# Additive attention with half-length key tiles for the first query blocks, and tanh units that begin after twelve of sixteen neighbourhood-attention rounds

## The chip, the cores and the metric

One NeuronCore of one Trainium2 chip. The metric is the time of one execution on the device, in microseconds (us). The profile is of one such execution; its times count from the first recorded instruction. The engines are TensorE (PE), VectorE (DVE), ScalarE (ACT), GpSimd (POOL) and SyncE (SP, which here only issues DMAs). Each runs its own list of instructions in order, and they wait for each other through semaphores.

## What is computed

Two images of 32 x 32 tokens with 128 channels, all in float32. Three layers follow one another:

```python
# 1: neighbourhood attention, 7 x 7, 8 heads of 16 channels
attn = einsum('bijnd,bijnpqd->bijnpq', q, k_neighbours) + bias
out = softmax(attn) @ v_neighbours
y = layernorm(x + (out @ proj_w + proj_b) * gate) * ln_g + ln_b
# 2: additive attention over all 1024 tokens of an image, 32 hidden units
t = layernorm(y)
q, k = t @ Wt, t @ Wx
e = (tanh(q[:, :, None, :] + k[:, None, :, :] + bh) * Wa).sum(-1) + ba
y = y + softmax(e) @ t
# 3: mixture of 8 experts, top 1, capacity 320
out = y + expert(layernorm(y)) * probability
```

The second layer needs 2 x 1024 x 1024 x 32 = 67 million tanh values. They are the largest work of the kernel.

## The kernel before

**Blocks.** The 2048 tokens are 16 blocks of 128 (`NB`), 8 to an image (`BPI`); blocks 0 to 7 are image 0.

**Rounds of the first layer.** A block takes two rounds (`NR` = 32; even heads, odd heads). Round `rho` is: scores on PE (L601), bias and row minimum on DVE (L1125), the exponential on ACT (L986), transposes of the probabilities on PE, their copies out of PSUM, and the product with the values on PE (L648). After a block's second round come the head sums, their inverse spread over the channels, the output projection and the gated sum `gate_heads` (L1188), which leaves the block in `y_all`. A round has 320 keys for most blocks and 256 for the first and the last block of an image.

**Layernorms.** Two layernorms stand between the first layer and the second. They are done for groups of blocks, and each is a chain of small instructions on DVE: `row_stats` (L1205, L1208), then `scale_start` and `scale_end` (L1214, L123 to L135), an inverse square root in 12 linked steps on 128 x 4 numbers. Scaling the rows themselves is on DVE (L1229, L1236) or on POOL (`scale_rows`, `weigh_rows`, `normal_rows`, L461 to L483). Then the tokens are transposed (`turn_tokens`, L757), copied to `xT`, and multiplied into keys (`key_half`, L762, copied to `k4` and left in PSUM too) and queries (`query_columns`, L769, copied to `q4`).

**Units of the second layer.** A unit `t` (0 to 127; 8 to a block, `CH`) is four columns of `q4` (each holds four queries, with their 32 hidden units, on the 128 partitions), each against the 1024 keys of the image: one tile of 128 x 4096 in a ring of three (`ring`, in `front`). POOL and DVE form the sums of key and query (`key_query_sums`, L507 and L1323): POOL reads the keys from SBUF, DVE from PSUM. In image 0 POOL makes two tiles of 1024 and two of 512, DVE two of 512; in image 1 POOL makes two of 1024 and one of 512, DVE one of 512 and one of 1024. ACT does one tanh over the whole tile (`hidden_units`, L1049). PE multiplies by `Wa` into banks 0 and 1 of PSUM (`energies`, L801); it waits for `h_ready`, and both makers of sums wait for `h_used` of three units earlier. PE may start a new block only when DVE has taken the energies of the last one out (`least_ready`, `least`, L1330).

**Finishing a block.** When the 8 units of block `p` are done: `least` on DVE, exponential on ACT (L1053), eight transposes (L813), copies (L1338), the product with the tokens (`attend`, L822), then `attended`, `normed`, `route` and `slotted` on DVE with three small products on PE, and on POOL an indirect DMA that puts the block's rows where their expert reads them (`scatter`, L515). These steps are spread over the ten steps behind the block's end (`query_block(t, phase)`).

**Order of the work.** It is written out by hand. First come the sixteen rounds of image 0 (`for rho in range(RPI)` on PE, ACT and DVE). Then comes a passage in which blocks 4 to 7 are normalised on DVE, image 1's queries and keys for the first layer are projected, and the keys and queries of image 0 for the second layer are made. Then one loop over steps `t` follows on each engine; step `t` holds unit `t`'s tanh and energies, the sums of unit `t + 2`, and whatever small functions give for `t`: rounds 16 to 31 begin at every third step,

```python
def begin(rho):
    return PACE * (rho - RPI - 1)
```

so at steps -3, 0, 3, ... 42. Blocks 8 to 11 are normalised in steps 29 to 38 (`middle`), blocks 12 to 15 in steps 49 to 58 (`late_rows`). After the loop the experts run (L926 to L946, L1079, L1519), in which nothing is changed.

**Memory.** Queries, keys and values of the first layer lie in `front` for image 0 and in `late` for image 1. `front` is also the ring, so no sum can be made before round 15 has been used up (`pv_done, RPI`).

## Time and profile before

| | |
|---|---|
| median of 3 runs | 742.11 us (741.74 to 746.65) |
| the profiled execution's own time | 744.08 us |
| its span, first to last instruction | 741.9 us |
| mean granted TensorE clock (1 is 2.4 GHz, 0.5 is 1.2 GHz) | 0.913 |
| first tanh of a unit starts | 109.79 us |
| last tanh ends | 659.9 us |
| busy share of the span: PE, DVE, ACT, POOL | 77%, 75%, 78%, 63% |

The span less the two tanh times leaves three parts: 109.8 us ahead of the units, 550.1 us of units, 82.0 us behind them. The time of an instruction on DVE, ACT or POOL is from its start to its end in the record; two that follow each other overlap a little, so that the distance from start to start is shorter (a tanh lasts 3.6 us and the next starts 3.5 us after it).

### The profile page before, as it was taken

The numbers are of one execution on the slowest core, as the hardware profiler recorded it, in microseconds if no ns is written. First come the engines' busy times: TensorE is split into PE (matmuls) and PEld (weight loads), VectorE is DVE, ScalarE is ACT, GpSimd is POOL, SyncE is SP. The second block draws the span as 40 slices with busy tenths as digits, with TensorE's granted clock in tenths as the row PEclk, the third lists the DMA queues.
The fourth block names the chain that finished last, engine by engine and source line by source line (L and its number), as shares of the span: only waits on it lengthen the run. The fifth ranks groups of instructions, "written<-read, shape, count | busy, mean of one in ns | idle before, by whom it ended". The sixth has DMA issues, their size and how long they took to land.

```text
span 741.9 us, 12240 instructions
## 1 busy us (share of the span) xinstructions
PE 570.2 (77%) x4496; PEld 272.5 (37%) x4496; DVE 555.0 (75%) x1444; ACT 577.5 (78%) x368; POOL 470.6 (63%) x539
## 2 busy tenths in 40 slices
PE   6999858798999868899447666766767668768994
PEld 3666423243434323343113131222222212328783
DVE  3768765768897768878987788798798786853356
ACT  3777539998999767899457899999999999960541
POOL 2000228976888668788835788788888886830464
PEclk9999968999999869999858899999999998986998
DMA  8500000000000000007000000000000000001400
GB/s 322 175 1 2 1 0 2 0 2 4 9 4 10 3 9 5 1 12 285 21 4 8 4 11 2 12 9 4 12 10 4 12 8 5 6 7 25 133 22 28
DMA packets 13819, 22.22 MB, mean 30 GB/s; under 512 B 1264, under 2 KB 11026, under 8 KB 12992
## 3 DMA queue, kind: packets, MB, share of 16 engines
q1 hardware_dynamic: 12352, 18.53, 7.3%
q0 software_dynamic: 1408, 2.91, 1.2%
q8 instruction: 36, 0.59, 0.3%
q14 instruction: 23, 0.19, 0.1%
HBM read 14.70 MB, written 7.37 MB: 30 GB/s over the span
## 4 chain that ended last, share of the span: by engine, by line
PE 36%; DVE 27%; issue 18%; ACT 13%; POOL 4%; DMA 0%; DVEq 0%; POOLq 0%; SPq 0%; ACTq 0%
PE ps L801 12%; ACT front L1049 11%; DVE front L1323 7%; POOL front L507 4%; PE ps L601 3%; PE ps L946 3%; PE ps L936 2%; PE ps L648 2%; PE ps L822 2%; DVE back L1125 2%; PE ps L630 2%; PE ps L639 2%; DVE lnw L134 1%; PE ps L813 1%; DVE rec L1362 1%
## 5 line engine op out<-in xcount | busy, mean ns | idle before, releaser
L507 POOL TENSOR_SCALAR front<-k,q 128x1024 f32<-128x1024 f32 (+1 forms) x448 | 410.9, 936 | 129.0 <-PE ps L801 110.7
L1049 ACT ACTIVATE front<-front 128x4096 f32<-128x4096 f32 x128 | 456.2, 3608 | 41.8 <-DVE front L1323 23.6
L801 PE MATMUL ps<-front,cst 128*32 128x512 f32 x2048 | 277.1, 648 | 74.8 <-ACT front L1049 61.1
L1323 DVE TENSOR_SCALAR front<-ps,q 128x512 f32<-128x512 f32 (+1 forms) x256 | 213.5, 877 | 34.6 <-PE ps L801 27.9
L801 PEld LDWEIGHTS ps<-front,cst 128*32 128x32 f32 x2048 | 53.1, 114 | 173.6 <-issue 85.2
L986 ACT ACTIVATE back<-back,mn 128x320 f32<-128x320 f32 (+1 forms) x128 | 62.5, 537 | 20.2 <-DVE mn L1125 20.2
L1125 DVE CUSTOM_DVE_ANT_0 back<-ps,back 128x320 f32<-128x320 f32 (+1 forms) x128 | 54.0, 468 | 12.8 <-PE ps L601 11.8
L464 POOL TENSOR_SCALAR y_all<-y_all,lny,lnc 128x128 f32<-128x128 f32 x8 | 3.5, 444 | 69.0 <-DVEq L1224 69.0
L1338 DVE COPY ptm<-ps 128x512 f32<-128x512 f32 x32 | 22.1, 689 | 30.1 <-PE ps L813 30.1
L1152 DVE COPY back<-ps 128x512 f32<-128x512 f32 x44 | 30.2, 687 | 16.3 <-PE ps L639 13.9
L639 PEld LDWEIGHTS ps<-cst,back 128*128 128x128 f32 x176 | 20.0, 150 | 44.0 <-issue 31.6
L832 PE MATMUL ps<-cst,rec 128*128 128x128 f32 x16 | 5.9, 371 | 38.0 <-DVE rec L1362 38.0
L822 PEld LDWEIGHTS ps<-x_one,ptm 128*128 128x128 f32 x256 | 31.4, 199 | 10.0 <-issue 8.8
L822 PE MATMUL ps<-x_one,ptm 128*128 128x129 f32 x256 | 34.3, 289 | 0.8 <-DVE ptm L1338 0.8
L515 POOL DMA_INDIRECT xbuf<-rec,slots x16 | 16.3, 1019 | 29.2 <-DVEq L119 25.9
L639 PE MATMUL ps<-cst,back 128*128 128x128 f32 x176 | 31.3, 303 | 2.2 <-DVE back L1152 2.0
L543 POOL DMA_INDIRECT out<-back,dest x20 | 19.9, 993 | 17.6 <-DVE back L1529 13.4
L630 PE MATMUL ps<-cst,back 128*128 128x128 f32 x176 | 27.3, 287 | 1.7 <-ACT back L993 1.7
L601 PE MATMUL ps<-late 32*128 32x320 f32 (+1 forms) x128 | 26.7, 494 | 2.5 <-DVE mn L1125 1.7
L813 PEld LDWEIGHTS ps<-cst,pm 128*128 128x128 f32 x128 | 14.7, 151 | 32.8 <-issue 19.2
L813 PE MATMUL ps<-cst,pm 128*128 128x128 f32 x128 | 22.9, 306 | 4.7 <-ACT pm L1053 2.0
L1072 ACT ACTIVATE front<-ps 128x384 f32<-128x384 f32 (+1 forms) x8 | 3.1, 434 | 29.8 <-PE ps L926 29.8
(140 smaller groups left out, 701.4 us busy)
## 6 DMA issues: line engine op xcount, KB each, us to landing
back<-in_w SPq DMA_DIRECT2D x2, 2048.0 KB, 10.3
xbuf<-rec SPq DMA_DIRECT2D x1, 2720.0 KB, 14.4
front<-xbuf SPq DMA_DIRECT2D x2, 720.0 KB, 7.2
back<-in_inner SPq DMA_DIRECT2D x1, 1280.0 KB, 9.8
back<-in_b SPq DMA_DIRECT2D x1, 1280.0 KB, 14.1
xT<-in_xT SPq DMA_DIRECT2D x4, 256.0 KB, 5.4
back<-in_top SPq DMA_DIRECT2D x1, 1024.0 KB, 6.8
back<-in_bottom SPq DMA_DIRECT2D x1, 1024.0 KB, 14.9
```

The source lines that it names most:

```text
L507: last = nc.gpsimd.tensor_scalar(ring[t % 3][:, c, lo:hi], k4[:, img * L + lo:img * L + hi], q4[:, m:m + 1], 1.0, ALU.add, ALU.mult)
L601: return nc.tensor.matmul(bank(to, 0, n), q_par[img][r][rows, at * P:(at + 1) * P], kT[img][rows, k0:k0 + n], start=True, stop=True)
L630: last = nc.tensor.transpose(bank(turn_bank(rho, c), g * P, (g + 1) * P), prob[r][:, g, c * P:(c + 1) * P], c_("ident"))
L639: last = nc.tensor.transpose(bank(4, g * P, (g + 1) * P), prob[rho % 2][:, g, c * P:(c + 1) * P], c_("ident"))
L801: last = nc.tensor.matmul(bank(half)[c * U:(c + 1) * U, :], c_("wa", U - QPG - QPG * s, 2 * U - QPG - QPG * s), ring[t % 3][:, c, half * 5 ...
L813: last = nc.tensor.transpose(bank(4, k * P, (k + 1) * P), pm[:, (4 * half + k) * P:(4 * half + k + 1) * P], c_("ident"))
L822: last = nc.tensor.matmul(bank(6, 2 * P, 2 * P + C + 1), ptm[:, k, :], x_one[:, p // BPI * BPI + k, :], start=(k == 0), stop=(k == BPI - 1))
L986: nc.scalar.activation(prob[r][:, g, 0:n], nlog[r][:, g, 0:n], ACT.Exp, bias=mn[r][:, g:g + 1], scale=-1.0).then_inc(p_ready, 1)
L1049: nc.scalar.activation(ring[t % 3], ring[t % 3], ACT.Tanh).then_inc(h_ready, 1)
L1125: nc.vector.tensor_tensor_reduce(out=nlog[r][:, g, 0:n], in0=bank(frm, 0, n), in1=btab[kind][:, 2 * g + r, :], scale=-1.0, scalar=3e38, op ...
L1152: nc.vector.tensor_copy(pts[rho % 2][:, c, :], bank(4)).then_inc(turn_copied, 1)
L1323: last = nc.vector.tensor_scalar(ring[t % 3][:, c, lo:hi], ps[:, at + lo:at + hi], q4[:, m:m + 1], None, ALU.add)
```

## The change

Four things are changed together.

1. **Twelve rounds first (`RS` = 12).** Only rounds 0 to 11 (blocks 0 to 5) run ahead of the loop. The other twenty begin at the steps of a table: rounds 12 to 15 at -6, -3, 0 and 2, rounds 16 to 23 every four steps from 7 to 35, rounds 24 to 31 every three from 38 to 59.
2. **Half the keys at a time.** The first four blocks of an image are worked in two passes. Units 0 to 15 take blocks 0 to 3 (four units each) against keys 0 to 511; units 16 to 31 take the same blocks against keys 512 to 1023; then blocks 4 to 7 follow as before with 8 units each. Image 1 does the same from unit 64 on. A half unit has eight columns of `q4` against 512 keys, again 128 x 4096. Its sums are eight tiles of 512: six on POOL and two on DVE in image 0, five and three in image 1. After the first pass `least` keeps the negated energies in `pmh` and their minimum in `nmh`; after the second one it takes the smaller of both minima, and ACT does two exponentials of 512 instead of one of 1024. The first pass of a block ends without the other finishing steps; those of blocks 0 to 3 follow each other every 4 units, behind units 19, 23, 27 and 31 (and 83 to 95).
3. **Layernorms and keys in other places.** Blocks 0 to 3 are normalised in rounds 8 to 11 (statistics, `scale_start` and `scale_end` of the first layernorm all stand in rounds 8 and 9) and not in rounds 9 to 15. Blocks 4 to 6 are normalised in steps 7 to 11 of the loop, on DVE and POOL, block 7 alone in steps 11 and 12, on DVE, in place of the passage between rounds and loop. Tokens and keys of blocks 4 to 7 follow at step 14 (`KEYS_1`), on PE and DVE; unit 16 is the first to need them. Blocks 8 to 11 now stand at steps 45 to 54 and blocks 12 to 15 at 66 to 75, the keys of blocks 8 to 11 at step 61 (`KEYS_2`).
4. **One store for queries, keys and values (`conv`)** instead of two, so that the ring is free from the start; image 1's projections stand in steps 4 to 6 (`ENTRY`), partly on DVE, its values in steps 7 to 9.

The core of the diff (the functions that only follow from it, such as the counts of semaphores, are left out):

```diff
-PACE = 3
+RS = 12
+BS = RS // 2
...
+BEGIN = dict(zip(range(RS, NR), [-6, -3, 0, 2] + [7 + 4 * k for k in range(8)] + [38 + 3 * k for k in range(8)]))
+ROWS_STEPS = (7, 8, 9)
+ENTRY = 4
+KEYS_1, TOKENS_2, KEYS_2 = 14, 58, 61
...
+for _img in range(B):
+    for _half in range(2):
+        for _k in range(BPH):
+            GROUPS.append(Group(_img * BPI + _k, _half, len(GROUPS) and GROUPS[-1].last + 1, CH // 2))
+    for _k in range(BPH, BPI):
+        GROUPS.append(Group(_img * BPI + _k, None, GROUPS[-1].last + 1, CH))
...
+def tiles_of_unit(u):
+
+    g = GROUPS[GROUP_AT[u]]
+    k = u - g.first
+    base = g.block * U
+    if g.half is None:
+        return [(c * L, 0, L, base + c * CH + k, k, c) for c in range(QPG)]
+    return [(n * HL, g.half * HL, HL, base + n % QPG * CH + 2 * k + n // QPG, 2 * k + n // QPG, n % QPG)
+            for n in range(2 * QPG)]
...
+        def pool_part(u, n):
+
+            g = GROUPS[GROUP_AT[u]]
+            if g.half is not None:
+                return (0, HL) if n < (6 if g.block < BPI else 5) else (0, 0)
+            if g.block < BPI:
+                return (0, L) if n < 2 else (0, HL)
+            return (0, L) if n < 2 else (0, HL) if n == 2 else (0, 0)
...
+                if t == 8:
+                    scale_rows(2, 4, 7)
+                    weigh_rows("lng", ALU.mult, 4, 7)
+                    weigh_rows("lnb", ALU.add, 4, 7, done=True)
+                if t == 11:
+                    normal_rows(2, 4, 7)
...
-            for rho in range(RPI):
-                if rho + 1 < RPI:
+            for rho in range(RS):
+                if rho + 1 < RS:
                     scores(rho + 1)
...
+                if t == KEYS_1:
+                    pe.wait_ge(n_ready, NG * (RPI + 2))
+                    turn_tokens(1, 2)
+                    query_columns(1, 3)
+                    pe.wait_ge(dve_sums, NEW_KEYS[1])
+                    key_half(1, 5)
...
+                if rho == 8:
+                    dve.wait_ge(y_ready, 3)
+                    row_stats(0, 3)
                 if rho == 9:
                     dve.wait_ge(y_ready, 4)
-                    row_stats(0, 2)
+                    row_stats(3, 4)
+                    scale_start(0, 4)
+                    scale_end(0, 4, ln_scale)
                 if rho == 10:
-                    row_stats(2, 4)
+                    dve.wait_ge(ln_rows, 1)
+                    row_stats(0, 4)
                 if rho == 11:
                     scale_start(0, 4)
...
-            row_stats(4, BPI - 1)
-            gated(BPI - 1)
-            dve.wait_ge(y_ready, BPI)
-            row_stats(BPI - 1, BPI)
-            scale_start(4, BPI)
-            scale_end(4, BPI)
-            normal_rows(y_all, 4, BPI)
-            weigh_rows(4, BPI)
-            row_stats(4, BPI)
-            scale_start(4, BPI)
-            scale_end(4, BPI)
-            normal_rows(x_all, 4, BPI)
-            dve.sem_inc(t_ready[1], 1)
+                    scale_end(0, 4, ln_last)
...
+                if t == project_step(6) + 1:
+                    dve.wait_ge(misc_read, misc_uses(t))
+                    row_stats(4, 7)
+                    scale_start(4, 7)
+                    scale_end(4, 7, ln_scale)
...
+                if g.half == 0:
...
+                    nc.vector.tensor_tensor_reduce(out=pmh[:, k, :], in0=bank(p % 2), in1=c_("ba").broadcast_to([P, HL]),
+                                                   scale=-1.0, scalar=3e38, op0=ALU.add, op1=ALU.min,
+                                                   accum_out=nmh[:, k:k + 1]).then_inc(least_ready, 1)
+                    return
```

How the lists of instructions move, at the places that matter. ACT ahead of its first tanh; before (`late` is the first layer's store of image 1):

```order
L999 ACTIVATE ots<-ps 128x256
L969 ACTIVATE late<-ps,sbq 128x512 x2
L974 ACTIVATE late<-ps,cst 128x512
L1003 ACTIVATE xT<-ps 128x512
L969 ACTIVATE late<-ps,sbq 128x512 x2
L1007 ACTIVATE k<-ps 128x512
L974 ACTIVATE late<-ps,cst 128x512
L1003 ACTIVATE xT<-ps 128x512
L1007 ACTIVATE k<-ps 128x512
L1044 ACTIVATE q<-ps,cst 128x256
L986 ACTIVATE back<-back,mn 128x256 x4
L1049 ACTIVATE front<-front 128x4096 x2
```

and after (L1067 are the exponentials of rounds 12 and 13, L1118 is the tanh):

```order
L1080 ACTIVATE ots<-ps 128x256
L1067 ACTIVATE back<-back,mn 128x320 x2
L1084 ACTIVATE xT<-ps 128x512
L1067 ACTIVATE back<-back,mn 128x320 x2
L1088 ACTIVATE k<-ps 128x512
L1145 ACTIVATE q<-ps,cst 128x128
L1067 ACTIVATE back<-back,mn 128x320 x4
L1118 ACTIVATE front<-front 128x4096 x2
```

Between the last round and the first tanh the projections of image 1 and the second half of tokens and keys are gone, and two rounds' exponentials stand there.

DVE at the layernorm of blocks 4 to 7; before, in the passage ahead of the loop (L119 ends a chain):

```order
L119 ISA
L1214 TENSOR_SCALAR lnh<-mvs 128x4
L125 TENSOR_SCALAR lnw<-lnh 128x4
L126 TENSOR_SCALAR lny<-lnw 128x4
L133 TENSOR_TENSOR lnw<-lny,lnh 128x4
L134 TENSOR_TENSOR lnw<-lnw,lny 128x4
L135 SCALAR_TENSOR_TENSOR lny<-lnw,lny 128x4
```

and after, in the loop, behind unit 9's sums (L1394) and ahead of unit 10's (L1205 is a copy of image 1's values, L1292 the heads of block 7):

```order
L1205 TENSOR_TENSOR conv<-ps,cst 128x32x16
L1292 COPY ots<-ps 128x256
L1296 BN_STATS bns<-y_all 128x6 x3
L1299 BN_AGGR mvs<-bns 128x2 x3
L122 ISA
L1305 TENSOR_SCALAR lnh<-mvs 128x3
L128 TENSOR_SCALAR lnw<-lnh 128x3
L129 TENSOR_SCALAR lny<-lnw 128x3
L136 TENSOR_TENSOR lnw<-lny,lnh 128x3
L137 TENSOR_TENSOR lnw<-lnw,lny 128x3
L138 SCALAR_TENSOR_TENSOR lny<-lnw,lny 128x3
```

The same chain stood alone before and stands between the sums of two units now, and what is queued behind it on DVE are sums for which ACT waits.

POOL's sums of one unit of image 0; before:

```order
L507 TENSOR_SCALAR front<-k,q 128x1024 x2
L507 TENSOR_SCALAR front<-k,q 128x512 x2
L507 TENSOR_SCALAR front<-k,q 128x1024 x2
L507 TENSOR_SCALAR front<-k,q 128x512 x2
L507 TENSOR_SCALAR front<-k,q 128x1024 x2
```

and after, at the layernorm of blocks 4 to 6; the 66 are the eleven units 0 to 10, the 18 units 11 to 13:

```order
L570 TENSOR_SCALAR front<-k,q 128x512 x66
L532 TENSOR_SCALAR y_all<-y_all,lny,lnc 128x128 x3
L122 ISA
L539 TENSOR_TENSOR y_all<-y_all,cst 128x384
L122 ISA
L539 TENSOR_TENSOR y_all<-y_all,cst 128x384
L570 TENSOR_SCALAR front<-k,q 128x512 x18
L549 TENSOR_SCALAR x_one<-y_all,lny,lnc 128x128 x3
```

A half unit is six instructions of 512 where a whole one is two of 1024 and two of 512, and the scaling of blocks 4 to 6 stands among them.

## Rows read from the trace of the kernel before

**Rows 1.** Head of the page: busy time of each engine and its share of the span

```profile
span 741.9 us, 12240 instructions
PE 570.2 (77%) x4496; PEld 272.5 (37%) x4496; DVE 555.0 (75%) x1444; ACT 577.5 (78%) x368; POOL 470.6 (63%) x539
```

**Rows 2.** Busy time by stretch: from:to, us, each engine (instructions), TensorE clock, DMA

```profile
18.00:84.00 66.00, 60.53 (x727) 42.52 (x728) 48.85 (x201) 45.06 (x97) 3.91 (x6) 0.97 0.17 54
84.00:109.80 25.80, 15.62 (x55) 6.84 (x55) 17.04 (x75) 8.94 (x17) 5.32 (x9) 0.76 0.00 0
109.80:177.20 67.40, 57.86 (x462) 23.19 (x462) 48.79 (x113) 66.28 (x38) 56.62 (x64) 0.93 0.01 2
177.20:250.70 73.50, 66.91 (x590) 29.91 (x594) 62.95 (x179) 69.19 (x41) 58.99 (x66) 0.96 0.02 7
250.70:336.80 86.10, 73.37 (x574) 31.18 (x566) 68.04 (x197) 67.54 (x38) 64.52 (x76) 0.88 0.02 6
336.80:421.80 85.00, 51.63 (x359) 18.77 (x362) 71.90 (x155) 59.61 (x19) 57.96 (x65) 0.80 0.18 70
421.80:541.00 119.20, 83.78 (x649) 29.58 (x641) 99.15 (x193) 116.66 (x36) 96.00 (x100) 0.96 0.02 8
541.00:659.90 118.90, 83.10 (x640) 29.62 (x638) 95.98 (x196) 116.98 (x37) 93.16 (x97) 0.96 0.02 7
```

**Rows 3.** Waits: engine and line, for whom, us in total, times, longest

```profile
POOL front L507 <- PE ps L801: 110.7, 75, 13.5
ACT front L1049 <- DVE front L1323: 23.6, 12, 8.6
ACT front L1049 <- POOL front L507: 18.0, 21, 2.6
```

**Rows 4.** ACT in order of time: start, us, engine line op, operands, count

```profile
109.79 7.14 ACT L1049 ACTIVATE front<-front 128x4096 f32<-128x4096 f32 x2 [0.94 <-POOL front L507]
129.87 1.00 ACT L986 ACTIVATE back<-back,mn 128x320 f32<-128x320 f32 x2
...
520.00 28.15 ACT L1049 ACTIVATE front<-front 128x4096 f32<-128x4096 f32 x8
```

**Rows 5.** DVE and POOL in order of time, rounds and the passage behind them

```profile
66.27 0.69 DVE L1144 COPY back<-ps 128x512 f32<-128x512 f32 x1 [0.28 <-PE ps L630]
66.88 0.16 DVE L1214 TENSOR_SCALAR lnh<-mvs 128x4 f32<-128x4 f32 x1
...
72.56 0.16 DVE L1223 SCALAR_TENSOR_TENSOR lnc<-mvs,lny 128x4 f32<-128x4 f32 x1
...
99.30 1.12 DVE L1229 TENSOR_SCALAR x_one<-y_all,mvs,lny 128x128 f32<-128x128 f32 x4
```

**Rows 6.** POOL in order of time: its last layernorm step, then three units' sums

```profile
87.18 1.74 POOL L481 TENSOR_SCALAR x_one<-y_all,lny,lnc 128x128 f32<-128x128 f32 x4 [9.93 <-DVEq L1224]
...
211.40 10.65 POOL L507 TENSOR_SCALAR front<-k,q 128x1024 f32<-128x1024 f32 x12 [1.20 <-PE ps L801]
```

**Rows 7.** Groups by shape: sums on POOL and DVE; count | busy, mean ns

```profile
L507 POOL TENSOR_SCALAR front<-k,q 128x1024 f32<-128x1024 f32 x256 | 283.4, 1119 | 129.0 <-PE ps L801 110.7 <-ACT q L1044 17.3
L507 POOL TENSOR_SCALAR front<-k,q 128x512 f32<-128x512 f32 x192 | 131.3, 692 | 0.0
L1323 DVE TENSOR_SCALAR front<-ps,q 128x512 f32<-128x512 f32 x192 | 137.5, 744 | 34.6 <-PE ps L801 27.9 <-ACT q L1044 4.7 <-DVE slots L1393 1.3
L1323 DVE TENSOR_SCALAR front<-ps,q 128x1024 f32<-128x1024 f32 x64 | 81.5, 1274 | 0.0
```

**Rows 8.** DVE in order of time in the layernorm of blocks 12 to 15

```profile
354.93 2.07 DVE L1214 TENSOR_SCALAR lnh<-mvs 128x4 f32<-128x4 f32 x1
...
361.19 7.01 DVE L134 TENSOR_TENSOR lnw<-lnw,lny 128x4 f32<-128x4 f32 x1
368.23 0.63 DVE L135 SCALAR_TENSOR_TENSOR lny<-lnw,lny 128x4 f32<-128x4 f32 x1
```

**Rows 9.** POOL in order of time over the same stretch

```profile
351.23 17.62 POOL L507 TENSOR_SCALAR front<-k,q 128x1024 f32<-128x1024 f32 x20
382.40 3.55 POOL L507 TENSOR_SCALAR front<-k,q 128x1024 f32<-128x1024 f32 x4 [13.55 <-PE ps L801]
```

461 lines of the change are left out of this document (264 added, 197 removed).

## The prediction

> **What bounds the kernel now.** I read the head of the page first [rows 1]: no engine is full, the busiest (ACT) is busy for 78% of the span. An average over stages with different limits says little, so I next read the busy times by stretch [rows 2], cut at the tanh of units 0, 16, 32, 48, 64, 96 and at the last one's end. They give three parts. Ahead of unit 0 lie 109.8 us, the last 25.8 of them (84.0 to 109.8) with every engine poorly used. Then come 550.1 us of units, in which ACT is the engine that should be full: a tanh starts every 3.51 us when nothing hinders it (eight take 28.15 us less the overlap, [rows 4]). The experts behind them are 82 us and stay as they are. In the unit stretches ACT's gaps, width less busy time [rows 2], are 1.1, 4.3, 18.6, 25.4, 2.5 and 1.9 us, together 53.8. Two stretches have nearly all of it: units 32 to 47, where blocks 8 to 11 are normalised, and 48 to 63, where 12 to 15 are. The list of waits says whom the tanh waited for: DVE's sums 23.6 us, POOL's 18.0, while POOL itself waits 110.7 us for PE [rows 3], so it has slack on the whole.
>
> Why a layernorm hurts there is seen in single instructions. A step of the chain on 128 x 4 numbers takes 0.16 us when POOL is idle [rows 5]. In the loop the same L134 took 7.01 us and L1214 2.07, and the next free one came only at 368.23 [rows 8]; all this while POOL ran twenty sums without a pause, from 351.23 to 368.85 [rows 9]. DVE's own sums stood queued behind, ACT waited for them up to 8.6 us [rows 3], PE fell idle and its clock with it: 0.80 of 2.4 GHz in that stretch against 0.96 in its neighbours [rows 2]. So DVE and POOL are the true limit of the stages with a layernorm.
>
> **The front, a gain.** In round 11 DVE's copy L1144 ends at 66.9 [rows 5]. After the change rounds 8 to 11 must also hold the whole normalisation of blocks 0 to 3. `scale_start` and `scale_end` are 2.5 us of chain, of which 66.88 to 72.7 shows both with a round between them [rows 5]; in round 9 both stand together, and against the slack of DVE in a round (66.0 less 48.85 us busy over 16 rounds, 1.1 each, [rows 2]) some 2 us remain. Then: copy of round 11 at 68.9, both chain pieces to 71.4, POOL's `normal_rows` 1.7 us (L481, [rows 6]) and two semaphores to 73.4. From there to the first tanh the path is transposes, copy, keys, queries, copies, POOL's sums: before, it went from 100.4 (end of L1229, [rows 5]) to 109.8 (first tanh, [rows 4]), 9.4 us. A half unit's sums on POOL are longer by 0.5 (below), and two rounds' exponentials stand on ACT on the way, 0.3. That gives a first tanh at 83.6; with rounding up for waits between the engines I take 84.0. **Term: -25.8 us** (22 to 30).
>
> **ACT's own work in the loop.** Sixteen units with two finished blocks are 58.5 us (half of 116.98, [rows 2]), without the finishing exponentials 56.4. A round adds four exponentials, two by two, each pair 0.9 us from the next tanh [rows 4], 1.8 in all, and about 1.6 with 256 keys. Three query copies move into the loop at 0.6. An exponential in two halves I take at 1.1 against 1.04 (between no dearer and 0.3 dearer for a second start). By stretches of 16 units: 65.0 (4 short rounds, copies), 68.0 (4 rounds, 4 finishes), 66.4 (5 rounds, 1), 67.3 (5, 2), 57.5 (none, 1), 59.7 (none, 3), 58.6, 58.5. Sum 501.0 against 496.3 before, which is 550.1 less the gaps. **Term: +4.7 us.** Were that all, the change would bring 21 us. The gaps decide.
>
> **POOL and DVE in a half unit.** A whole unit of image 0 keeps POOL 3.55 us (three in 10.65, [rows 6]). By mean durations two of 1024 and two of 512 are 3.62 [rows 7], so the overlap is 2%; six of 512 are 4.15, less 2% 4.07. That is above a tanh's 3.51, and about ACT's share of a unit with its rounds (65.0/16 = 4.06, 68.0/16 = 4.25). In image 1 it is five of 512, 3.39. DVE has 2 x 0.744 as before in image 0, and 3 x 0.744 = 2.23 against 2.02 in image 1 [rows 7]. So POOL loses nearly all its slack in units 0 to 31, and that is the state in which rows 8 show DVE starved.
>
> A page speaks of this too. The Trainium skill, "GPSIMD Engine Reference", Specifications, says that GpSimd shares its SBUF interfaces with VectorE and contends with instructions that read two SBUF inputs or run in a two-port mode. The trace agrees as far as it goes (L134 has two SBUF inputs: 7.01 us beside POOL, 0.16 without); by that rule a chain moved from beside an idle POOL to beside a full one would cost more than its own length, which is the side that I take below from the rows alone; without it the chains of blocks 4 to 7 would fit beside the tanh and the time would be nearer to rival 1's.
>
> **The gaps, stretch by stretch (after).**
> - Units 0 to 15: now two more normalisations, blocks 4 to 6 in steps 7 to 11 and block 7 in 11 and 12. Without disturbance they are four chains of 2.5 us with statistics and scaling, some 14 us of DVE; before, this ran beside an idle POOL in the 25.8 us passage. In the loop a normalisation brought gaps of 18.6 and 25.4 us. For these two, with fewer rows but four chains too, and POOL scaling three blocks in between, I take 14 beyond the old 1.1. At step 14 tokens and keys of blocks 4 to 7 are made two steps before unit 16: from a finished normalisation to q4 it took from 100.4 to 106.2 before (the 9.4 us less POOL's 3.6), while tanh 14 and 15 cover some 5 of those and of POOL's next 4; I take 4.5. Sum 20 (8 to 32).
> - Units 16 to 31: fewer rounds (every 4 steps instead of 3), but finishes begin every 4 units. A finish costs DVE (95.98 less 32 x 2.02 of sums) / 4 = 7.8 us [rows 2, 7]. DVE has 24 of sums, about two finishes, four rounds at some 4.2 (62.95 less 24 and 16, over 5.3, [rows 2]): 57, below ACT's 68. Gap as before plus a little for POOL: 5.
> - Units 32 to 47: three finishes (those of the half blocks come late), five rounds: 24 + 23 + 21 = 68 of DVE against 66.4 of ACT; before, 63 against 69 left 4.3. I take 7.
> - Units 48 to 63: blocks 8 to 11 are normalised, rounds every 3 steps: the load of old units 32 to 47, 18.6.
> - Units 64 to 79: blocks 12 to 15, the old 25.4, plus DVE's third sum tile, 27.
> - Then 2.5, 4 (finishes in a row, with 2.23 of sums) and 1.5.
> Sum 85.6 against 53.8: **+31.8 us.** The units then take 501.0 + 85.6 = 586.6, against 550.1.
>
> **Small edits.** PE no longer waits for `least` between half blocks (alternate banks), the memsets of a second store fall away, the loads of the expert weights start after step 64 instead of 47, and there is room of 60 steps for 5 MB that took 15 us: nothing. Scatters of blocks 0 to 3 follow each other after 4 units, 16 us, and DVE waits for that of two blocks ago: hidden.
>
> **Sum.** The profiled execution took 744.1 us (span 741.9). 744.1 - 25.8 + 4.7 + 31.8 = 754.8. The median of the runs shown is 2.0 below the profiled one, so 752.8, say **753 us**, 1.5% slower. About 1% (7.4 us) is what a measurement of this kernel tells from no change.
>
> **Rivals.**
> 1. *The gaps do not grow* (faster). The layernorm of blocks 4 to 7 falls into steps in which DVE has no finishes to do, and ACT's work per unit is 4.06 us with only rounds beside it; rounds at 4 steps relieve what follows. The total of gaps stays near 60: 501 + 60 = 561, end at 645 instead of 660, 727 us. For it: in units 0 to 15 ACT waited for 1.1 us only, with POOL busy for 84% [rows 2]. Against: rows 8, and that the chains' 14 us are added to a DVE that is at 72% there already.
> 2. *POOL never pauses in half units* (slower). With 4.07 us per unit POOL is then the bound of units 0 to 31, and each small SBUF instruction of DVE waits as L134 did. It begins to decide where POOL's work per unit passes ACT's. Four stretches of half units lose some 5 us more each: 773 us. For: rows 8 and 9. Against: POOL's instructions are shorter (512), and DVE got in between single ones at times (0.63 us, [rows 8]); the ring stops POOL after three units.
> 3. *Only the hand-over is cheap*: as forecast, but the new normalisations cost 10 less: 742 us, no change.
> 4. *The first tanh does not come early* (the change does not do what it says): the chain of blocks 0 to 3 in rounds 9 to 11 is exposed, each round waiting for POOL's scaling; first tanh at 95, 764 us.
>
> **Chances.** Forecast 0.42 (own range 744 to 764), rival 1 0.20, rival 2 0.18, rival 3 0.12, rival 4 0.08. The range of 8 in 10 reaches down to rival 1's upper part, 731, and up to 775. Faster by over 1% (below 734.7): rival 1 nearly whole, 0.19. Within 1%: rival 3, the forecast's lower part, the rest of rival 1: 0.27. Slower: 0.54.
>
> **What the new profile would show.** First tanh near 84; tanh 16 at 84 + 85 = 169, tanh 32 at 242, tanh 48 at 315, tanh 64 at 401, tanh 80 at 486. In steps 7 to 13 instructions of the chain (then L137, L1305) far above 0.16 us, POOL without a pause beside them, a hole before tanh 16. If ACT's waits for DVE and POOL stay at the 41.6 us of rows 3, rival 1 is right; if the first tanh is at 90 or later, the front's term is wrong; if POOL is busy for over 95% of units 0 to 31 and DVE's small instructions are long all over it, rival 2.

## The result and the profile after

The changed kernel takes 780.6 us (median of 4 executions, 773.5 to 792.4) against 742.0 before. The execution of 792.4 us is over 1.5% above the fastest and counts as slow; without it the median is 777.4 us and the ratio 1.047, 95% interval 1.037 to 1.058. I had forecast 753 us with a range up to 775. It is slower, as forecast, but by 35 to 39 us and not by 11. All readings of "after" below are of one profiled execution, and it is this one of 792.4 us, with a span of 790.2. Run 1 of the experiments gives a second profile of the same code at 787.3 us. The last 81.8 us of the span, behind the last tanh, are the experts, as long as before.

The same cut by stretches as in [rows 2], at the tanh of units 0, 16, 32, 48, 64, 80, 96, 112 and at the last one's end. Columns: from:to, width in us, busy us and instructions of PE, PEld, DVE, ACT, POOL, TensorE clock, DMA share, GB/s:

```profile
18.00:85.70 67.70, 56.20 (x602) 38.30 (x602) 47.09 (x189) 40.42 (x86) 10.15 (x17) 0.92 0.16 53
85.70:184.40 98.70, 72.39 (x490) 28.26 (x494) 76.84 (x173) 65.32 (x37) 68.26 (x105) 0.81 0.00 1
184.40:262.40 78.00, 63.62 (x498) 26.06 (x491) 62.09 (x144) 68.01 (x38) 64.85 (x96) 0.89 0.02 5
262.40:346.90 84.50, 70.95 (x557) 31.72 (x556) 68.86 (x198) 68.97 (x40) 59.77 (x67) 0.90 0.03 8
346.90:433.80 86.90, 71.84 (x608) 32.14 (x608) 76.16 (x207) 68.14 (x39) 64.36 (x78) 0.92 0.02 6
433.80:511.90 78.10, 49.49 (x335) 16.64 (x327) 63.65 (x161) 58.17 (x18) 57.20 (x84) 0.83 0.19 76
511.90:577.40 65.50, 41.88 (x312) 14.21 (x316) 48.69 (x106) 60.43 (x23) 53.29 (x78) 0.91 0.02 5
577.40:650.10 72.70, 52.55 (x355) 19.82 (x347) 59.54 (x129) 59.55 (x20) 50.27 (x53) 0.83 0.03 9
650.10:708.40 58.30, 40.77 (x318) 14.42 (x318) 44.71 (x97) 58.26 (x19) 43.98 (x46) 0.97 0.02 7
```

The first tanh comes at 85.7 (before 109.8), so the front gives 24.1 us. The units then take 622.7 us instead of 550.1. ACT's busy time in them adds up to 506.9, so its gaps are 115.8 us (111.7 in run 1), where before they were 53.8 and I had forecast 85.6. Width of each stretch of 16 units, forecast and measured:

| units | 0-15 | 16-31 | 32-47 | 48-63 | 64-79 | 80-95 | 96-111 | 112-127 |
|---|---|---|---|---|---|---|---|---|
| before | 67.4 | 73.5 | 86.1 | 85.0 | 60.8 | 58.5 | 58.9 | 60.0 |
| forecast | 85.0 | 73.0 | 73.4 | 85.9 | 84.5 | 62.2 | 62.6 | 60.0 |
| after | 98.7 | 78.0 | 84.5 | 86.9 | 78.1 | 65.5 | 72.7 | 58.3 |
| ACT's gaps, after | 33.4 | 10.0 | 15.5 | 18.8 | 19.9 | 5.1 | 13.1 | 0.0 |

The waits of after that answer to [rows 3], and one that was small before (engine and line, for whom, us in total, times, longest):

```profile
POOL front L570 <- PE ps L861: 138.9, 61, 9.2
...
ACT front L1118 <- DVE front L1394: 50.2, 27, 6.0
...
PE ps L888 <- DVE rec L1452: 38.7, 12, 7.8
...
ACT front L1118 <- POOL front L570: 29.3, 20, 4.6
```

The tanh's waits for the sums went from 41.6 to 79.5 us, two thirds of them for DVE. POOL waits for PE even longer than before, so it is no fuller: in units 0 to 15 it is busy for 68.3 of 98.7 us. Where it hurts is seen in single instructions. After, in order of time, around unit 5:

```profile
99.64 14.70 POOL L570 TENSOR_SCALAR front<-k,q 128x512 f32<-128x512 f32 x22
...
107.56 3.62 ACT L1118 ACTIVATE front<-front 128x4096 f32<-128x4096 f32 x1
107.70 6.78 DVE L1246 COPY rzx<-rz 128x256 f32<-128x256 f32 x1
116.19 0.50 PEld L635 LDWEIGHTS ps<-xT,cst 128*128 128x128 f32 x2 [0.38 <-issue]
...
120.01 0.69 ACT L1055 ACTIVATE conv<-ps,sbq 128x512 f32<-128x512 f32 x1 [8.83 <-PE ps L635]
120.59 3.61 ACT L1118 ACTIVATE front<-front 128x4096 f32<-128x4096 f32 x1
```

A copy of 128x256 between two places in SBUF ends when POOL's unbroken run of sums ends (99.64 + 14.70 = 114.34; 107.70 + 6.78 = 114.48; the view shows the last 22 sums of the run). Behind it stand DVE's own sums and a result that PE needs; PE's projections for image 1 come late, ACT's query copy is in ACT's queue ahead of the tanh and waits 8.83 us. From one tanh (107.56) to the next (120.59) are 13.0 us.

The same copy of the next block, beside unit 17, is held too:

```profile
186.32 14.03 POOL L570 TENSOR_SCALAR front<-k,q 128x512 f32<-128x512 f32 x21
...
191.72 8.78 DVE L1246 COPY rzx<-rz 128x256 f32<-128x256 f32 x1
...
201.90 3.62 ACT L1118 ACTIVATE front<-front 128x4096 f32<-128x4096 f32 x1 [1.57 <-DVE front L1394]
```

Again it ends with POOL's run (200.35 and 200.50). ACT's two gaps behind it, ahead of units 20 and 21, are 1.6 and 3.7 us.

From unit 9 on stands the new normalisation:

```profile
137.03 0.16 DVE L137 TENSOR_TENSOR lnw<-lnw,lny 128x3 f32<-128x3 f32 x1
...
146.98 8.03 POOL L570 TENSOR_SCALAR front<-k,q 128x512 f32<-128x512 f32 x12 [1.21 <-PE ps L861]
147.12 0.56 DVE L136 TENSOR_TENSOR lnw<-lny,lnh 128x3 f32<-128x3 f32 x1
...
151.72 0.63 DVE L137 TENSOR_TENSOR lnw<-lnw,lny 128x3 f32<-128x3 f32 x1
152.38 0.63 DVE L138 SCALAR_TENSOR_TENSOR lny<-lnw,lny 128x3 f32<-128x3 f32 x1
...
155.43 3.62 ACT L1118 ACTIVATE front<-front 128x4096 f32<-128x4096 f32 x1 [6.00 <-DVE front L1394]
```

As long as POOL's twelve sums run, each step of the chain takes 0.63 us, hardly less than one sum (8.03 / 12 = 0.67); the same step took 0.16 at 137.03, when POOL had none under way (its run before had ended at 136.7). The tanh waited 6.0 us for the DVE sums behind the chain.

What is held has one thing in common: all its operands are in SBUF. DVE's instructions with an input in PSUM (its sums, the copies out of PSUM, bias and minimum) are never held. Each of the 20 profiles of this document has some 700 of them, and none took more than 0.02 us above the median of its line and shape, whatever POOL did beside it.

For the experiments I use the excess of DVE's small instructions: for each line and shape the time above its 10th percentile, summed over a stretch. It is 18.7 us in units 0 to 15 of after, against 2.4 before (such a sum moves by up to 0.8 us with the choice of what counts as small).

### The profile page after: what moved, and what is told of

The parts are those of the page before. It is cut to its first block, busy times and chain, and to the rows that moved or that the text cites. A ratio compares the mean times of both kernels' runs of the same rounds, so it can differ in the third digit from the quotient of the medians.

```text
span 790.2 us, 12536 instructions
## 1 busy us (share of the span) xinstructions
PE 594.5 (75%) x4512; PEld 280.5 (35%) x4512; DVE 589.6 (75%) x1535; ACT 573.5 (73%) x363; POOL 504.8 (64%) x673
## 3 DMA queue, kind: packets, MB, share of 16 engines
HBM read 14.70 MB, written 7.37 MB: 28 GB/s over the span
## 4 chain that ended last, share of the span: by engine, by line
DVE 36%; PE 34%; issue 17%; ACT 8%; POOL 1%; DVEq 1%; POOLq 0%; ACTq 0%
PE ps L861 12%; DVE front L1394 10%; ACT front L1118 7%; PE ps L719 3%; DVE back L1216 3%; PE ps L671 2%; PE ps L1032 2%; PE ps L710 2%; PE ps L1022 2%; DVE back L1243 2%; PE ps L872 2%; DVE rzx L1246 1%; PE ps L700 1%; DVE lny L138 1%; PE ps L904 1%
## 5 line engine op out<-in xcount | busy, mean ns | idle before, releaser
L570 POOL TENSOR_SCALAR front<-k,q 128x512 f32<-128x512 f32 (+1 forms) x576 | 442.1, 787 | 154.3 <-PE ps L861 138.9
L1118 ACT ACTIVATE front<-front 128x4096 f32<-128x4096 f32 x128 | 458.4, 3610 | 79.8 <-DVE front L1394 50.2
L861 PE MATMUL ps<-front,cst 128*32 128x512 f32 x2048 | 294.3, 680 | 46.7 <-ACT front L1118 42.3
L1394 DVE TENSOR_SCALAR front<-ps,q 128x512 f32<-128x512 f32 (+1 forms) x288 | 217.7, 802 | 24.9 <-PE ps L861 22.3
L1067 ACT ACTIVATE back<-back,mn 128x320 f32<-128x320 f32 (+1 forms) x128 | 62.6, 537 | 38.0 <-DVE mn L1216 38.0
L719 PE MATMUL ps<-back,conv 128*32 128x128 f32 x704 | 31.4, 318 | 36.2 <-issue 27.0
L1243 DVE COPY back<-ps 128x512 f32<-128x512 f32 x54 | 37.1, 687 | 18.0 <-PE ps L710 14.7
L710 PEld LDWEIGHTS ps<-cst,back 128*128 128x128 f32 x216 | 25.0, 152 | 58.0 <-issue 39.4
L710 PE MATMUL ps<-cst,back 128*128 128x128 f32 x216 | 39.1, 308 | 8.5 <-DVE back L1243 8.5
L671 PE MATMUL ps<-conv 32*128 32x320 f32 (+1 forms) x256 | 41.9, 476 | 2.4 <-DVE mn L1216 2.4
L719 PEld LDWEIGHTS ps<-back,conv 128*32 128x32 f32 x704 | 21.5, 125 | 51.9 <-issue 50.5
L613 POOL DMA_INDIRECT out<-back,dest x20 | 19.8, 989 | 18.5 <-DVE back L1662 13.9
L671 PEld LDWEIGHTS ps<-conv 32*128 32x128 f32 x256 | 16.3, 188 | 33.5 <-issue 25.2
```

The lines of the kernel that those rows point to most:

```text
L570: last = nc.gpsimd.tensor_scalar(ring[u % 3][:, at + lo:at + hi], k4[:, img * L + k0 + lo:img * L + k0 + hi], q4[:, m:m + 1], 1.0, ALU.add ...
L671: return nc.tensor.matmul(bank(to, 0, n), q_par[r][rows, at * P:(at + 1) * P], kT[rows, k0:k0 + n], start=True, stop=True)
L710: last = nc.tensor.transpose(bank(4, g * P, (g + 1) * P), prob[rho % 2][:, g, c * P:(c + 1) * P], c_("ident"))
L719: last = nc.tensor.matmul(bank(6, r * P, (r + 1) * P)[g * HP:(g + 1) * HP, :], vals[:, value_block(j, c), 2 * g + r, :], pts[r][:, c, g * ...
L861: last = nc.tensor.matmul(bank(to)[c * U:(c + 1) * U, :], c_("wa", U - QPG - QPG * row, 2 * U - QPG - QPG * row), ring[t % 3][:, at:at + H ...
L1067: nc.scalar.activation(prob[r][:, g, 0:n], nlog[r][:, g, 0:n], ACT.Exp, bias=mn[r][:, g:g + 1], scale=-1.0).then_inc(p_ready, 1)
```

## The experiments

Each run has the kernel before beside it on the same chip; its ratio is to that. Medians of before were 744.1, 743.9, 745.9, 744.9, 744.7 and 745.8 us in the six sets of runs. Stretches are read from one profiled execution each.

**1. The changed kernel once more.** 

> The changed kernel once more, for a second profile and a tighter ratio. Its four runs lay between 773.5 and 792.4 us, those of the kernel before between 741.7 and 746.7. If the loss comes from a race for the SBUF interface between GpSimd's sums and VectorE's small instructions (theory A), it depends on where each falls, and the spread stays 1% or more; if it is plain work (theory B: more instructions on VectorE, in a fixed order), the runs should agree within 0.5%. Both: 777 us, give or take 8.

788.2 us (781.4 to 789.5), ratio 1.057 (1.050 to 1.064), 7.6 us above the median of the first four executions and above the 777 plus or minus 8 that both theories gave. The spread is 1% here and 2.4% over all eight, as theory A had it. First tanh 86.6; stretches 95.1, 78.1, 84.4, 88.3, 77.9, 63.1, 71.8, 60.0. The medians of the two sets of four lie 1% apart, so the runs below are compared with both, and their stretches count for more than their times. Most of the spread is in units 0 to 15: in later runs whose edit does not touch those units they took between 85.9 and 98.7 us. Units 32 to 47 took 80.0 to 84.5 us, units 80 to 95 62.8 to 65.5.

**2. The reciprocal written straight into its spread form, from PSUM**, without the copy L1246:

```diff
-link(nc.vector.reciprocal(rz[:, :], bank(7, 0, NH)))
-nc.vector.tensor_copy(rzx..., rz[:, :, None].broadcast_to([P, NH, HP]))
+link(nc.vector.reciprocal(rzx..., bank(7, 0, NH)[:, :, None].broadcast_to([P, NH, HP])))
```

> The spread of the inverse head sums is one reciprocal that reads PSUM, in place of a reciprocal into SBUF and a copy from SBUF to SBUF (L1246), which in the changed kernel once took 6.78 us beside sixteen back-to-back sums of GpSimd. Same result. Theory A: the 16 us by which L1246 is too long in units 0 to 31 go, at least half of them from the end: 762 to 769 us. Theory B: one instruction of 0.3 us less for each of 16 blocks, mostly off the path: 774 to 777 us.

802.6 us, ratio 1.074 (1.066 to 1.083). Both theories missed, because the edit brought a cost of its own (RECIPROCAL of 128x256, DVE, by shape; count | busy, mean ns):

```profile
L1246 DVE RECIPROCAL rzx<-ps 128x256 f32<-128x256 f32 x16 | 28.0, 1752 | 1.2 <-PE ps L743 0.8 <-DVE osum L1353 0.2
```

The reciprocal's time goes by elements: 1752 ns for 256, 0.2 us for 8. In the front this put the first tanh at 98.9, and units 32 to 47 took 94.8 us instead of 84.4. Still, the distance of tanh 5 and 6 shrank from 13.0 to 5.9 us, and units 0 to 31 took 164.9 us instead of 173.2. The part in units 0 to 15 may be chance (see the end of run 9); that in units 16 to 31 is not: 72.5 us, where the eight profiles without an edit in these units have 78.0 to 78.8. The held copy is a real cost; this is no way to save it.

**3. Five sums on POOL.** In the half units of image 0 POOL does five of the eight sums and DVE three:

```diff
-return (0, HL) if n < (6 if g.block < BPI else 5) else (0, 0)
+return (0, HL) if n < 5 else (0, 0)
```

> In the half units of image 0 GpSimd makes five of the eight sums of 512 and VectorE three (before: six and two). GpSimd then needs 3.35 us for a unit in place of 4.02 and pauses between units; VectorE gets 32 x 0.74 = 24 us more work. Theory A (starved by a GpSimd that never pauses): same or faster, 765 to 777 us, with fewer long small instructions on VectorE in units 0 to 31. Theory B (VectorE has too much work): slower, 785 to 795 us.

778.0 us (777.5 to 779.0), ratio 1.045 (1.041 to 1.050): 10 us less than run 1 and 2.6 less than the first median, though DVE has 32 x 0.744 = 24 us more to do. L1246's excess in units 16 to 31 fell from 8.8 to 0.5 us, the two gaps of 1.6 and 3.7 us behind it went to nothing, and later gaps in the stretch took back 2.3 of these 5.3. Theory A, about a microsecond above its range: DVE was held more than it was full.

**4. The chains of blocks 4 to 7 cut short.** Each `scale_start` and `scale_end` pair of these blocks is replaced by

```diff
-scale_start(4, 7)
-scale_end(4, 7, ln_scale)
+link(nc.vector.tensor_scalar(lny[:, a], mvs[:, a, 1], 1e-5, 0.5, ALU.add, ALU.mult))
+link(nc.vector.scalar_tensor_tensor(lnc[:, a], mvs[:, a, 0], -1.0, lny[:, a], ALU.mult, ALU.mult))
```

> In the normalisations of blocks 4 to 6 and of block 7 the twelve linked steps of the inverse square root are left out (one instruction stands for them), four times; statistics and scaling stay, so this part of the computation is missing. It prices the chains inside the loop. Alone they would be 4 x 12 x 0.2 = 9.4 us of VectorE. Theory A: each step costs one sum of GpSimd, 0.63 us, so up to 25 us less, 755 to 765 us, all of it in units 0 to 15. Theory B: 4 to 8 us less, 769 to 773 us.

775.5 us, ratio 1.042 (1.037 to 1.047), 12.7 less than run 1 and 5.1 less than the first median. By time that is theory B or something between the two. Units 0 to 15 take 78.4 us, below all that this stretch took with its chains. But in this profile the copy beside unit 5 was not held. The like-for-like figure is the profile of run 9's last kernel, with the chains and without that hold: 85.9 us. So the roots of the four chains cost some 7.5 us, not the 16.7 that run 1 suggests.

**5. Half-unit shapes alone, on the kernel before:**

```diff
+cut = [lo, L // 2, hi] if hi - lo == L and t % (BPI * CH) < BPI * CH // 2 else [lo, hi]
+for lo, hi in zip(cut, cut[1:]):
     last = nc.gpsimd.tensor_scalar(...)        (and the same on DVE)
```

> The kernel before, with its order of work untouched, but the key-and-query sums of units 0 to 31 and 64 to 95 cut to the shapes that half units have: POOL writes its 1024-wide sums as two of 512 (six instructions of 512 instead of two of 1024 and two of 512 in image 0, five instead of three in image 1), DVE the 1024-wide one of image 1 as two of 512. Same numbers come out. Theory A (the shapes cost only what rows 7 give: POOL 4.07 us a unit instead of 3.55, DVE 2.23 instead of 2.02): units 0 to 31 grow by 2 to 6 us, units 64 to 95 by 0 to 2, together 3 to 8 us, ratio 1.004 to 1.011. Theory B (rival 2 of the prediction: with POOL at 4.07 us a unit it never pauses and DVE starves in every stretch of half units, 5 us more in each of four stretches): 15 to 25 us, ratio 1.02 to 1.034, with small DVE instructions far above their 0.16 us all over units 0 to 31.

768.1 us (767.0 to 768.6), ratio 1.033 (1.028 to 1.037). This is the size of theory B: 24 us from shapes alone, with no instruction of another kind. But not by its mechanism. Units 0 to 31, where POOL is nearest to full, give only 7.3 of them, with POOL busy for 64.3 of 71.7 and 66.0 of 76.5 us; units 64 to 95 give 14.1 (67.3 and 66.0 instead of 60.8 and 58.5), where POOL has much slack.

**6. POOL's shapes alone, only in units 64 to 95** (the same cut, on POOL, for `64 <= t < 96`). 

> The kernel before, with only POOL's two 1024-wide sums per unit written as two of 512 each, and only in units 64 to 95 (image 1); DVE keeps its shapes. With both engines' shapes changed these 32 units had taken 67.3 + 66.0 us instead of 60.8 + 58.5. Theory A (POOL's gapless run of five, 3.39 us instead of 2.93, holds DVE's row scaling of each finish for as long as it lasts): 62 to 67 us for each of the two stages, the time up by 5 to 12 us, ratio 1.007 to 1.016, and the 128x128 scaling of rows four times held by 1.5 us or more. Theory B (DVE's third sum, 2.23 us a unit instead of 2.02, did it): each stage within 1.5 us of before's, the time within 3 us.

758.1 us, ratio 1.017 (1.011 to 1.022): 12 us, stretches 67.5 and 65.6. Theory A. Four instructions carry most of it: the row scaling in each finish, here and, below, in the kernel before (DVE in order of time):

```profile
451.91 3.75 DVE L1364 TENSOR_SCALAR rec<-rec,mv,sy 128x128 f32<-128x128 f32 x1
485.52 3.13 DVE L1364 TENSOR_SCALAR rec<-rec,mv,sy 128x128 f32<-128x128 f32 x1
518.38 3.75 DVE L1364 TENSOR_SCALAR rec<-rec,mv,sy 128x128 f32<-128x128 f32 x1
550.95 3.27 DVE L1364 TENSOR_SCALAR rec<-rec,mv,sy 128x128 f32<-128x128 f32 x1
```

```profile
449.34 0.46 DVE L1362 TENSOR_SCALAR rec<-rec,mv,sy 128x128 f32<-128x128 f32 x1
478.96 1.24 DVE L1362 TENSOR_SCALAR rec<-rec,mv,sy 128x128 f32<-128x128 f32 x1
507.86 0.47 DVE L1362 TENSOR_SCALAR rec<-rec,mv,sy 128x128 f32<-128x128 f32 x1
537.66 1.11 DVE L1362 TENSOR_SCALAR rec<-rec,mv,sy 128x128 f32<-128x128 f32 x1
```

It takes 3.5 us on average instead of 0.8, about as long as POOL's five sums of one unit (5 x 0.69). Four times 2.65 are 10.6 of the 13.8 us that these stretches grew, and ACT's new gaps stand there: in the two units behind each of the first three it idles for about 3 us, where before it idled for none.

**7. Wider instructions for half units:** the first four sums on POOL as two TENSOR_TENSOR of two queries each.

```diff
+for n in (0, 2):
+    nc.gpsimd.tensor_tensor(ring[...] as [P, 2, HL], k4[...] broadcast over n, q4[:, m:m + CH + 1:CH] broadcast over keys, ALU.add)
```

> The changed kernel, with the first four 512-wide sums of each half unit on POOL written as two TENSOR_TENSOR of two queries each (128x1024, both operands broadcast), so that a half unit is two wide and two narrow instructions, as a whole unit of image 0 was. Same numbers come out. What such an instruction takes on POOL no row shows. Theory A (number and length of POOL's instructions are what half units cost, and a wide TENSOR_TENSOR costs about what a wide TENSOR_SCALAR does, 1.12 us): the time falls by 10 to 20 us to 765 to 775. Theory B (TENSOR_TENSOR with two SBUF inputs is at least half slower than TENSOR_SCALAR, 1.7 us or more): POOL needs 4.8 us or more a half unit, is the bound of the 64 half units, and the time rises by 30 us or more.

859.7 us, ratio 1.154. Theory B: the instruction takes 1.90 us where TENSOR_SCALAR of the same size takes 1.12.

```profile
L572 POOL TENSOR_TENSOR front<-k,q 128x1024 f32<-128x1024 f32 x128 | 240.4, 1899 | 73.4 <-PE ps L869 58.9 <-DVE k L1501 6.9 <-ACT q L1153 5.5
```

**8. Runs 3 and 4 together.** 

> The changed kernel with both earlier edits: POOL does five instead of six 512-wide sums of a half unit in image 0 (alone 10 us faster), and the four inverse square roots of the normalisation of blocks 4 to 7 are left out, so that these rows are scaled wrongly (alone 13 us faster). Theory A (one cause, a DVE held by POOL's gapless runs: either edit takes away part of what the other does): 767 to 773. Theory B (the two are separate costs and add up): 764 or less, units 0 to 15 at 73 us or less.

764.5 us, ratio 1.025 (1.019 to 1.031). By medians the parts add up: 10.2 + 12.7 = 22.9 us below run 1, and both together 23.7. By the ratios it is 19.0 and 23.5. Theory B's total is met within its rounding, its 73 us for units 0 to 15 is not: 76.2, with a DVE excess of 4.5. Each of these differences is good to some 5 us only, and the profiles of runs 3, 4 and 8 all lack the hold beside unit 5. So two separate costs are likely, not shown.

**9. What makes units 96 to 111 slow** (72.7 us; in all runs that leave them alone 71.3 to 72.7). Eight runs. First TensorE's clock, 0.83 in after and 1.0 before ([rows 2] give 0.96 with the next stretch), by filler ahead of the energies of units 92 to 108:

```diff
+for _ in range(4):
+    nc.tensor.matmul(bank(5, 0, P), c_("ident"), c_("tri"), start=True, stop=True)
```

> The changed kernel with four matmuls of 128 columns on a free bank ahead of the energies of each of units 92 to 108; they compute nothing that is used. It asks whether TensorE's half clock (energies 3.64 us a unit at it, against about 2) makes units 96 to 111 take 72 us instead of 58.5. Theory A (the clock does): granted clock of the stretch rises above 0.95, the 16 units fall to 59 to 64 us, the whole time falls by 8 to 13 us. Theory B (PE waits for the finish of a query block on DVE, and the low clock is the consequence): the stretch stays at 69 to 74 us, the whole time within 3 us of the changed kernel's.

788.5 us, ratio 1.059; 73.1 us for the stretch, though the granted clock of its slow part rose from 0.87 to 0.92. Theory A asked for above 0.95, so the clock is not cleared by this run alone, but it gave back nothing. The last run of this section answers it: over all of the stretch the clock is 0.94 here, at 73.1 us, and 0.92 there, at 62.9.

Then PE's order, with `turn_normed`, `logits` and `counts` moved from ahead of `energies(t, 0)` to behind `energies(t, 1)`. 

> The changed kernel with three PE pieces of a block's finish (the transpose of the normalised rows, the gate's logits, the counts) moved in PE's order from ahead of the step's energies to behind them; nothing else moves. In the changed kernel PE waited for DVE's normalised rows up to 7.2 us, 14.1 us in all in units 96 to 111, with the energies that the ring of three waits for queued behind. Theory A (this in-order wait is what the closer finishes, every 4 units instead of 8, cost): units 96 to 111 fall from 72 to 60 to 66 us, units 32 to 47 and 64 to 95 by 2 to 5 together, the time by 8 to 16 us. Theory B (DVE's load and the order of its own queue set the pace; PE's wait only shows it): the stretch stays within 2 us and so does the time, or gets longer as the finish itself comes a step later.

829.7 us, ratio 1.117. The stretch stays at 71.8, and units 16 to 63 get slower (units 48 to 63: 104.2); that there the queue of DVE waits for these results, with the rounds' work behind them, is my reading and not tested. Theory B by its numbers. It does not clear the in-order wait, though: PE's wait for the rows is still there, 12.0 us in three waits, as the move put the pieces behind the energies of one step and left them ahead of the next step's.

Then a 512-wide sum per unit moved from DVE to POOL in units 88 to 107. 

> The changed kernel with one 512-wide sum per unit moved from DVE to POOL in units 88 to 107, where finishes follow every 4 units (half units: POOL six instead of five; whole ones: two of 1024 and two of 512 instead of two and one). Same numbers come out. It asks what makes units 96 to 111 take 72 us instead of 58.5, after a higher clock alone (0.92 for 0.87) gave nothing. Theory A (DVE's load: 43.0 us busy in 51, sums and two overlapping finishes): units 96 to 111 fall to 62 to 68 us, the time by 3 to 9 us. Theory B (POOL's gapless runs hold the small steps of the finish, as in image 0): the stage rises to 74 to 80 us, the time by 2 to 8 us.

787.7 us, ratio 1.058; the stretch 71.4. Neither. DVE's excess rose from 7.4 to 10.3 us, and took back part of what it had less.

Then one engine's work taken away at a time: in the finish the root's eight steps become one, `link(nc.vector.tensor_scalar(sy[:, :], sv[:, :], 1.5, None, ALU.subtract))`. 

> The changed kernel without the inverse square root in the finish of every query block: eight dependent DVE steps on 128x1 (two of 0.15 us, three pairs of 0.27 and 0.21) are replaced by one, so the rows that the experts get are scaled wrongly. DVE has about 1.7 us less work and waiting per finish. Units 32 to 47 (84.4 us where I forecast 73.4) and 96 to 111 (71.8 where I forecast 62.6) hold three finishes each. Theory A (DVE's queue sets the pace in both): 3 to 6 us less in each of these two stages, 1 to 4 in units 48 to 63, the time down by 8 to 16 us. Theory B (something else does, PE in units 32 to 47 at 83% busy, or the ring's round trip): no stage moves by more than 1.5 us.

766.4 us (one execution 775.4, the profiled one; four others 766.0 to 766.4), ratio 1.030 (1.025 to 1.034). Units 96 to 111 fell by 1.0, 32 to 47 by 4.0, 48 to 63 by 3.7. The time is 14.2 us below the first median, as theory A had it, and 21.8 below run 1, which is more. The stretches don't settle it: units 32 to 47 took 80.0 us in two later runs as well, without any edit there.

In `attend`, `for k in range(0, BPI, 4)` instead of all eight. 

> The changed kernel with two of the eight matmul pairs in which a finish applies the softmaxed weights (128x129 columns each), six left out for every block, so that its output is wrong. PE has 1.5 us less work per finish, DVE and ACT have all of theirs. Theory A (PE's work sets the pace of units 32 to 47, where it is busy for 70 of 84 us): 2 to 5 us less there, the time down by 3 to 10 us. Theory B (DVE does): no stage moves by more than 1.5 us, the time within 3 us.

780.7 us (769.2 to 785.5), ratio 1.041. The time lies within the spread of the unedited kernel and decides nothing. Units 32 to 47 are at 84.2, 96 to 111 at 72.2: PE's work in a finish is not the pace of either.

In units 88 to 107, one sum less on POOL (`and not (88 <= u < 108 and n == 2)` in its loop). 

> The changed kernel; in units 88 to 107 POOL leaves out one of its 512-wide sums per unit (the tanh then reads an old tile there, so the output is wrong), DVE keeps all its own. POOL has 0.69 us less a unit and pauses more. The stage is units 96 to 111, 71.8 us where 62.6 were forecast. Theory A (DVE is held by POOL's gapless runs): the DVE excess of 7.4 us in the stage at least halves and the stage falls to 63 to 68 us. Theory B (DVE's own load, 43 of 51 us): the stage stays within 1.5 us.

777.4 us, ratio 1.044; the stretch 70.3. POOL is busy for 42.9 instead of 50.4 us there, DVE's excess fell by a third, and the stretch gained 1.5. Theory B's size.

And one less on DVE. 

> The changed kernel; in units 88 to 107 DVE leaves out one of its 512-wide sums per unit (old data in the tile, so the output is wrong), POOL keeps all its own. DVE has 0.74 us less a unit, 12 us over units 92 to 107. Theory A (held by POOL): the freed time is mostly given back, as with the missing root, and the stage of units 96 to 111 falls by 3 us at most. Theory B (DVE's own load): it falls from 71.8 to 60 to 66 us.

781.2 us, ratio 1.047; the stretch 70.2. DVE is busy for 52.1 instead of 59.1 us, and the stretch gained 1.6. Theory A's size. So neither the load nor the hold of DVE is the main cost of the stretch. One wait had stayed as it was through all of these, PE's for the normalised rows (12.0, 11.7, 11.4 us). The last run gives it a step of slack:

```diff
+def late_block(t, phase):
+    return next((p for p in range(NB) if PEND[p] + 1 + phase + (p >= BPI) == t), None)
-p = query_block(t, 6)        (and 7, 8, on PE and on DVE)
+p = late_block(t, 6)
```

> The changed kernel; in the finishes of image 1 the transpose of the normalised rows, the logits and the counts, on PE and on DVE, come one step later (seventh, eighth and ninth step after the block instead of sixth to eighth), so that PE asks for DVE's normalised rows a whole step after DVE was given them. PE stood 12.0 us at that place in units 96 to 111, and hardly less (11.4, 11.7) when DVE or POOL had 7 us less work. Same numbers come out. Theory A (the hand-shakes of PE and DVE, one per step with two finishes under way, set the pace of units 96 to 111; the wait for the rows is the longest of them): the stage falls from 71.8 to 62 to 67 us, the time by 4 to 9 us. Theory B (the wait only moves to another hand-shake, since each step has one in both directions): the stage stays within 2 us.

772.7 us (768.3 to 784.5), ratio 1.037 (1.029 to 1.044). The stretch takes 62.9 us, 8.9 less. Theory A. With the stretch before it the gain is 7.2 us, as one gap of 4.4 us now stands at unit 95. The time fell by 15.5 us from run 1, but other stretches of this profile were short by chance, so it proves nothing here. The two stretches, run 1 first:

```profile
573.60:645.40 71.80, 50.01 (x355) 20.02 (x347) 59.13 (x129) 59.52 (x20) 50.40 (x53) 0.89 0.03 10
```

```profile
561.40:624.30 62.90, 43.68 (x317) 16.34 (x315) 54.72 (x126) 58.59 (x19) 50.10 (x53) 0.92 0.03 11
```

The waits of the same stretch, run 1:

```profile
PEld ps L888 <- DVE rec L1452: 14.1, 3, 7.2
ACT front L1118 <- DVE front L1394: 12.1, 10, 2.1
PE ps L888 <- DVE rec L1452: 12.0, 3, 6.3
```

and with the finish a step later:

```profile
PEld ps L866 <- ACT front L1123: 21.9, 12, 4.0
PE ps L866 <- ACT front L1123: 17.8, 11, 3.9
```

PE now waits for the tanh, as it should, and not for DVE. With a finish every 4 units two of them are under way in most steps up to 102. In one step DVE does `attended` of one block and `slotted` of the one before, then its sums, and only in the next step the root and the scaling of the first (`normed`); PE has by then reached the transpose of these rows and stands there, with the energies that free the ring queued behind. Before, with finishes 8 units apart, two met only at their ends, and PE's waits for the rows were 1.4 us each in this stretch.

This run shows something else by chance. Its units 0 to 15 are unchanged, but took 85.9 us, since the copy beside unit 5 that was held in after came through (DVE and POOL in order of time):

```profile
103.76 10.13 POOL L575 TENSOR_SCALAR front<-k,q 128x512 f32<-128x512 f32 x15
...
107.76 0.32 DVE L1251 COPY rzx<-rz 128x256 f32<-128x256 f32 x1
```

0.32 us instead of 6.78, in the middle of a run of sums of the same kind; from tanh 5 to 6 it then took 5.0 us instead of 13.0. Eleven profiles have the same code up to here. In seven the copy took 6.8 us, in one 2.2, in three 0.3 to 0.4. So this hold is met or missed by chance. The one beside unit 17 is not: it took 8.8 us in all eleven, and 0.8 in both runs with five sums on POOL. The chance hold is worth 8 us, against 19 between the fastest and the slowest execution of the changed kernel; the fastest was not profiled, so that it lacked the hold is only likely.

**10. The kernel before, with a sum moved from POOL to DVE in units 46 to 61:**

```diff
+if c == 1 and 46 <= t < 62:
+    lo = L // 2                                  (POOL)
-for c in range(2, QPG):
+for c in range(1 if 46 <= t < 62 else 2, QPG):   (DVE)
```

> The kernel before, with one 512-wide sum per unit moved from POOL to DVE in units 46 to 61 only, where two normalisations run beside the sums (POOL 1024 + 3 x 512 wide instead of 2 x 1024 + 2 x 512; DVE three of 512 instead of two). Same numbers come out. Theory A (DVE's small instructions are held while POOL runs without a pause; the run of POOL, not DVE's load, makes the 85.0 us of units 48 to 63): the excess of 21 us over free durations in that stage at least halves, the stage falls to 73 to 80 us, the time to 732 to 739. Theory B (DVE, busy for most of that stage, is full: 16 x 0.744 = 11.9 us more work for it): the stage grows by 4 to 12 us, the time is 748 to 756.

738.0 us (737.1 to 741.9), ratio 0.993 (0.990 to 0.996). It beats both kernels. The time is in theory A's range, its mechanism is met in sign but not in size: the excess in units 48 to 63 fell from 21.0 to 13.9 us and did not halve, the stretch from 85.0 to 83.1, the one before it from 86.1 to 83.4.

A second sum moved in units 52 to 59 (`c == 0 and 52 <= t < 60`, likewise). 

> The kernel before with the edit that made it 0.7% faster (one 512-wide sum per unit from POOL to DVE in units 46 to 61), and in units 52 to 59, where most steps of the two normalisations fall, a second one: POOL four of 512, DVE four of 512. Same numbers come out. Theory A (DVE held by POOL's gapless runs is still the larger cost there, with 13.9 us of excess left in units 48 to 63): that stage falls from 83.1 to 77 to 81, the time to 733 to 737. Theory B (DVE is now full: 8 x 0.744 = 6.0 us more for it): the stage is 84 to 88, the time 739 to 744.

737.7 us (735.1 to 741.1), ratio 0.991 (0.988 to 0.994): no difference to the first. The excess fell on, to 8.9 us, the stretch to 81.9; but the one before it is at 87.0. Neither theory. The best version is before with one of these, 0.7 to 0.9% faster.

## Why the prediction failed

The direction was right, the front too; the gaps were too small, and the time lies above the range. The profiled execution is 37.6 us above the 754.8 of my sum: 30.2 of them are gaps of ACT, 5.9 ACT's own work, 1.7 the front.

- *The front*, forecast -25.8: measured -24.1 (85.7) and, in run 1, -23.2 (86.6). Right: the chain of blocks 0 to 3 ended on DVE at 73.7, forecast 71.4, and what follows took 12.0 us instead of 12.6. Rival 4 is out.
- *ACT's own work*, forecast +4.7: measured 506.9 less 496.3, +10.6. Of the miss of 5.9, 2.6 are in units 32 to 47 (69.0, forecast 66.4).
- *Gaps*, forecast 85.6: measured 115.8. This is the term that failed, in four of its stretches; three are explained, the fourth is open. The step behind it that was wrong: I let POOL hold the chains of the layernorms only, and priced everything else on DVE by its load. The runs show two holds of a copy that is in no chain (8 and 5 us) and an in-order wait between PE and DVE (9 us).
  - Units 0 to 15, forecast 20 (8 to 32), measured 33.4. I counted 14 for the two normalisations; run 4 puts the roots of their chains at 7.5 (78.4 against 85.9). The keys of blocks 4 to 7 were counted at 4.5, and the gap ahead of unit 16 is 4.6. What I had left out is a hold of something that is in no chain: one copy of 128x256, some 8 us, met or missed by chance. Without it the stretch has gaps of 20.8 us.
  - Units 16 to 31, forecast 5, measured 10.0. The next hold of the same copy, beside unit 17, makes 5.3 of them, in every profile that has six sums on POOL and the copy. Runs 2 and 3, which take it away, bring the stretch down by 5.6 and 3.3 us.
  - Units 96 to 111, forecast 4, measured 13.1. I priced finishes in a row by DVE's load. Loads were not it: 7 us less on DVE or POOL gave 1.6 and 1.5 us, one step of slack 8.9.
  - Units 32 to 47, forecast 7, measured 15.5. The cause stays open. PE's work in a finish is not it; DVE's may be (no_finish_root), but unchanged code varied by as much (80.0 and 84.4 us). That three finishes overlap there as well was not tried, since the steps that the shift needs are taken by the rounds there.
  - Units 64 to 79, forecast 27, measured 19.9, gave some back.
- *The step "POOL and DVE in a half unit"* failed in kind. I priced half units by their sum of durations, 0.5 us each on POOL, and took 24 us of shapes for nearly nothing. Runs 5 and 6 show that what counts is beside which small instruction POOL's run falls. How much of the 24 us stands in after cannot be read off: over units 64 to 95, where run 5 lost 14.1, after is 3.1 us below what I had forecast with other causes in it.
- *Rivals 1 and 3* fall: the gaps did not stay near 60 us, and the new normalisations were not cheap. ACT's waits for DVE and POOL went to 79.5 us, not 41.6.
- *Rival 2* (773 us, "POOL never pauses, DVE starves") is the nearest, and its effect is there in units 0 to 31. Its condition is not: POOL is busy for 69% and 83% of them, not 95%. POOL needs no lasting fullness to hold DVE; one run of some five units (30 sums in each of the two holds) is enough, and the ring lets it make up three after every stall.
- Copies and scalings from SBUF to SBUF are held as well as the chains (6.78 against 0.32 us, 3.5 against 0.8), and nothing that reads PSUM is. I had looked for holds in the chains alone; L1246 and the row scaling belonged on the list too. The Trainium skill, "GPSIMD Engine Reference", Specifications, names contention with VectorE instructions that have two SBUF inputs or run in a two-port mode. The traces agree for the steps with two SBUF inputs (L137, 0.63 against 0.16 us). Whether the copy and the scaling run in that mode no run here shows.
- *Two readings of my rows* were wrong. The clock of units 48 to 63, 0.80, stands between 0.88 and 0.96, not between two of 0.96 [rows 2]. And the step at 368.23 was not free: it took 0.63 us, four times its 0.16 [rows 8]. Neither enters the sum.

## What to carry over

List every SBUF-to-SBUF instruction of DVE that will stand beside an unbroken run of POOL, not only the chain that is moved, and price each as if held until POOL pauses; the sums queued behind it count, not its own length. Splitting POOL's instructions cost more here than their fixed part (24 us, where 3 to 8 were expected of the durations), as it changes which instructions of DVE fall beside its runs. When periodic work comes at half the distance, look for steps in which two copies of it meet in one in-order queue ahead of something another engine waits for, and give that wait a step of slack before taking work away.

## What was not expected of the hardware

- A DVE instruction of 0.3 us was held for 6.8 us, or not at all, by the same code in two executions, beside unbroken runs of POOL both times. The same instruction 12 units later was held for 8.8 us in every one of eleven.
- Steps of 128x3 took 0.63 us each beside POOL's 512-wide sums, and 0.16 without. Instructions with an input in PSUM were never held.
- RECIPROCAL on DVE takes 1752 ns for 128x256 and 0.2 us for 128x8: 6 to 7 ns an element. It took 1.75 us in the front too, with POOL idle, so that is no hold. A copy of the same 256 took 0.3 us.
- TENSOR_TENSOR on POOL, 128x1024, took 1.90 us, TENSOR_SCALAR 1.12.
